# Moving four small copy groups on ScalarE behind a pair's exponentials in a fused attention, state-space and expert kernel

## The reference

```
Q = (x_text @ Wq) as 4 heads of 32;  K = (x_vision @ Wk) as 4 heads of 32
scores = Q K^T / sqrt(32)                       # per head 128 x 2048
topv, topi = top_k(scores, 32)
attn = softmax(topv) scattered to topi, zero elsewhere
attn_mean = attn.mean(over heads)               # 128 x 2048 per batch
c_t = attn_mean @ (x_vision @ Wv)               # 128 x 512 per batch
x = layernorm(x_text) * (1 + g * scale(c_t)) + g * shift(c_t)
y = s4d(x, ...)                                 # a convolution, its kernel computed from dt, A, C
```

## Time and profile before

| | |
|---|---|
| median of 3 runs | 776.59 us (776.24 to 779.22) |
| the profiled execution, device time | 776.36 us |
| its span, first to last instruction | 774.5 us |
| mean granted TensorE clock | 0.916 of full |
| busy: PE, DVE, ACT, POOL | 676.0, 366.7, 268.4, 234.1 us |
| PE busy in 84 to 115, 157 to 187, 187 to 209 us | 17.75 of 31, 25.71 of 30, 10.83 of 22 us |
| PE busy in 300 to 774 us | 449.78 of 474 us |

### The profile page before, as it was taken

How to read it: one execution, slowest core, us unless ns; L and a number is a source line. 1 busy time by engine, 2 the same in 40 slices (tenths; PEclk the granted TensorE clock), 3 DMA queues, 4 the chain that set the end, 5 groups by cost and what they waited for, 6 DMA issues and landing times.

```text
span 774.5 us, 10077 instructions
## 1 busy us (share of the span) xinstructions
PE 676.0 (87%) x3848; PEld 316.6 (41%) x3848; DVE 366.7 (47%) x1179; ACT 268.4 (35%) x564; POOL 234.1 (30%) x146
## 2 busy tenths in 40 slices
PE   4967669888378799999999999999699999999997
PEld 1423235334244354444444444455544333333343
DVE  5998769978998235570003350534661111001114
ACT  1866868779688110013210002444111001111010
POOL 2499668858977910000000000000140000000012
PEclk9977676868569999999999999999699999999999
DMA  9971320802706750014014023002958999999924
GB/s 296 289 271 52 108 83 2 271 1 76 291 0 222 213 239 19 1 41 176 0 50 167 0 82 135 1 1 74 361 201 311 389 379 344 373 373 371 384 81 135
DMA packets 63521, 132.94 MB, mean 172 GB/s; under 512 B 8368, under 2 KB 18544, under 8 KB 62960
## 3 DMA queue, kind: packets, MB, share of 16 engines
q1 hardware_dynamic: 59072, 122.91, 44.1%
q0 software_dynamic: 1920, 6.29, 2.8%
q10 hardware_dynamic: 2480, 3.08, 1.2%
HBM read 121.86 MB, written 8.32 MB: 168 GB/s over the span
## 4 chain that ended last, share of the span: by engine, by line
PE 67%; ACT 10%; DVE 7%; POOL 6%; DMA 4%; issue 3%; SPq 2%; DVEq 0%; POOLq 0%
PE PS L1696 7%; PE PS L1671 7%; PE PS L1492 7%; PE PS L1512 7%; PE PS L1410 6%; PE PS L1264 4%; PE PS L1529 4%; PE PS L1691 4%; PE PS L1676 4%; PE PS L1297 3%; DMA AR<-in_ctxT 3%; DVE AR L1010 2%; PE PS L1314 2%; PE PS L1526 2%; SPq L290 2%
## 5 line engine op out<-in xcount | busy, mean ns | idle before, releaser
L422 POOL TENSOR_TENSOR RS<-VE,CST 128x1 f32<-128x1 f32 (+1 forms) x18 | 11.2, 623 | 267.6 <-DVE VE L919 265.3
L1297 PE MATMUL PS<-AR,WK 128*128 128x512 f32 x96 | 55.8, 738 | 17.2 <-DMA AR<-in_ctxT 17.1
L956 DVE MAX8 KA<-AR 128x8 f32<-128x64 f32 x512 | 66.4, 211 | 0.8 <-ACT AR L607 0.8
L1235 DVE COPY AR<-PS 128x512 f32<-128x512 f32 (+1 forms) x9 | 5.9, 668 | 124.3 <-PE PS L1264 124.3
L574 POOL DMA_INDIRECT AR<-expert_rows,SLU x8 | 8.4, 1050 | 180.9 <-DMA expert_rows<-XT 178.8
L1696 PE MATMUL PS<-AR,TT 128*32 128x512 f32 x512 | 59.5, 593 | 1.4 <-issue 1.3
L1314 PE MATMUL PS<-AR,QT 32*128 32x512 f32 x128 | 45.1, 790 | 16.8 <-ACT AR L607 13.5
L1671 PE MATMUL PS<-AR 128*32 128x512 f32 x512 | 58.0, 594 | 1.1 <-ACT AR L870 0.6
L1492 PE MATMUL PS<-TT,AR 128*128 128x512 f32 (+2 forms) x144 | 55.5, 546 | 3.3 <-ACT TT L798 3.3
L1410 PE MATMUL PS<-AR 128*128 128x512 f32 x128 | 56.1, 594 | 0.9 <-ACT AR L770 0.6
L1512 PE MATMUL PS<-AR 128*128 128x512 f32 x128 | 55.5, 593 | 0.9 <-ACT AR L807 0.9
(11 more groups left out here) (293 smaller groups left out, 1197.4 us busy)
## 6 DMA issues: line engine op xcount, KB each, us to landing
AR<-in_w SPq DMA_DIRECT2D x32, 2048.0 KB, 12.4
AR<-in_ctxT SPq DMA_DIRECT2D x16, 768.0 KB, 7.6
AR<-in_ctx SPq DMA_DIRECT2D x16, 768.0 KB, 7.8
AR<-in_W SPq DMA_DIRECT2D x2, 4096.0 KB, 12.9
token_rows<-AR SPq DMA_DIRECT2D x1, 2560.0 KB, 10.1
X<-in_x SPq DMA_DIRECT2D x2, 1024.0 KB, 5.5
AR<-AR POOLq DMA_DIRECT2D x8, 256.0 KB, 3.4
AR<-in_W_film_in SPq DMA_DIRECT2D x4, 512.0 KB, 10.5
```

The costliest lines, as they stand in the source:

```text
L956: last = eng.max(CAND[i % 2][:, n, :], s[:, n * G // NCH:(n + 1) * G // NCH])
L1297: last = mm(PS[:, 4 + n % 2, :], WK[:, j, :], CXT[slot][:, j, :], start=j == 0, stop=j == KV - 1)
```

## The change

ScalarE's code is changed, no other engine's. In the even rounds 2, 4 and 6 the copies of the next batch's key chunks 2 and 3 stood at the round's end, and in rounds 4 and 6 `attended(q - 2)` followed them. Both now stand in the odd round that follows, behind that round's exponentials and ahead of its score copies. Round 0 keeps its two key copies where they were. `attended(2)`, in round 7 behind the magnitudes, stays too. No instruction is added or taken away.

```diff
                 if 2 <= m:
                     exponentials(m - 1)
                 if late:
+                    if q and q + 1 < B:
+                        context_keys(q + 1, (2, 3))
+                    if q >= 2:
+                        attended(q - 2)
                     if m + 1 < NPH:
                         scores(m + 1, (0, 1))
...
                         step_turns(q)
                     else:
                         exponentials(0)
-                    if q + 1 < B:
-                        context_keys(q + 1, (2, 3))
                     if m == 0:
+                        context_keys(1, (2, 3))
                         for b in range(1, B):
                             text_columns(b, (5, 7)[b % 2])
...
                         link(eng.activation(TM[:, :], TM8[:, :], ACT.Copy))
-                    if q >= 2:
-                        attended(q - 2)
```

## The result

| | before | after |
|---|---|---|
| median of 13 runs each | 776.73 us (775.36 to 779.24) | 780.29 us (779.32 to 783.3) |
| ratio, 95% interval | | 1.0047 [1.0036, 1.0057] |
| profiled execution, device time / span | 776.36 / 774.5 us | 782.19 / 780.4 us |

The changed kernel is slower by 0.47%, some 3.6 us, where 1.7 us were forecast. The sign was right and the time lies inside the stated range, but the loss is twice the forecast.

A forecast was written before the change was run, and what follows sets the result against it. TensorE was taken to bound the kernel, with ScalarE on the path in rounds 3, 5 and 7. -1.3 + 3.3 - 0.3 = +1.7 us on 776.36 gave 778.1; own range 776.9 to 779.4, wider 774.8 to 780.6.

The forecast's parts named there:

- Round 3, -1.3: Round 3: exponentials start earlier without the key copies ahead of them, a gain of 1.3 us.
- the two cases of the prediction, 0.83 and 1.71: Round 3: gain of 0.83 us with the eight transposes at the low clock, 1.71 at the high one.
- the bound of 2.44: Round 3: the most it can give, 2.44 us, VectorE's wait for the exponentials ahead of its masking.
- Round 5, +3.3: Round 5: TensorE waits at the CC transposes, then runs scores and transposes at the low clock, 3.3 us later.
- Round 7, -0.3: Round 7: masking starts 0.35 us earlier, the sines still wait for GpSimd, later copies stay hidden; gain 0.3 us.
- a sign that it is wrong: Round 7: the last exponentials waiting for L642 would show the prediction wrong.
- with 0.2 to spare: Round 7: L642 ends at 236.55, ahead of the last exponentials at 236.77, so it stays hidden.
- a context product that keeps the low clock longer: Round 7 rival: context product at the low clock longer outlasts its 0.2 us cover, 780.5 us; chance 0.14.
- The rest, 0: Outside the three rounds: no DMA moved, instruction counts and durations unchanged, no term in the sum.

The follow-up runs named there:

- e1: Changed kernel with TensorE's CC transposes of batches 0 and 1 moved behind the next pair's first scores; 0.9979 of the kernel before.
- e2: Changed kernel with only the key copies moved, `attended` back at its old place ahead of the exponentials; 0.9999 of the kernel before.
- e6: Changed kernel with round 5's CC transposes behind the first scores and batch 1's attended context back ahead of the exponentials; 0.9956 of the kernel before.
- e4: Changed kernel with 20 unused products in TensorE's idle time of round 5, ahead of the CC transposes; 0.9977 of the kernel before.
- e5: Changed kernel with batch 1's attended context back ahead of the exponentials, so round 7 is ordered as before; 1.0019 of the kernel before.
- e7: Changed kernel with three tiny VectorE instructions ahead of round 7's masking of head 12, to start it later; 1.0044 of the kernel before.
- e8: Changed kernel with 20 unused TensorE products in round 5 and batch 1's attended context back ahead of the exponentials; 0.9946 of the kernel before.
- e9: e8 with 10 more unused products in TensorE's idle time of round 3; 0.9962 of the kernel before.
- e3: Changed kernel with only `attended` moved, the key copies back at their old place ahead of the exponentials; 1.0063 of the kernel before.

## Why the prediction was right or wrong, step by step

- **Round 3, -1.3.** Measured -0.84 to -0.87 in both profiles of the changed kernel and in e1, e2 and e6; in e4, e5 and e7, with the same order at this place, it was -1.58 to -1.71. These are the two cases of the prediction, 0.83 and 1.71, one for each level of the clock at the eight transposes. A value between them, near the mean that I took, came only in e8 (-1.43), where the level fell in the midst of the transposes (1.38 us). With the clock held (e9) it is -2.56, where GpSimd binds, as the bound of 2.44 had it.
- **Round 5, +3.3.** Measured +3.1. The step itself, that TensorE waits at the CC transposes and then does in a row at the low clock what it did beside the exponentials, was right to 0.2 us: 164.09 for the transposes against 165.03 less the 0.94 that round 3 had given. One piece of its evidence was none: behind the wait of 5.37 us in the earlier trace rows stood only transposes that were not ready either, so it couldn't show that TensorE keeps its order. The 5.16 us in the changed kernel do, with scores standing ready behind them, which e1 runs at once when they stand first. e1, e3 and e4 show that order and clock make it together: the order alone taken away gives 4.2, the clock alone 6.1.
- **Round 7, -0.3.** This step failed. It measured +0.85 and +0.50 up to the last exponentials, and 0.9 more behind them. The last exponentials followed L642 directly, which the prediction had named as a sign that it is wrong. The prediction let the masking gain 0.35 and gave every instruction its old length, "with 0.2 to spare". But that gain (0.47 us against the subtraction, from 0.30 behind to 0.17 ahead) put the masking first, the subtraction became 2.05 longer, and the sines that were to wait for GpSimd as before waited for a later GpSimd. e5 and e7 show it. Of the two figures +0.50 is the one with the CC transposes at the high clock, +0.85 the one with them at the low. The rival that I had put at this place, a context product that keeps the low clock longer, was not the cause: the product took 10.59 us in the first profile, at the high clock, and 12.82 in the second, whose last exponentials came sooner.
- **The rest, 0.** In the profiles 0.9 and 2.7 us more passed from the last exponentials to the last context product. 0.9 of it is the change: it lies ahead of the last transposes (24.2 against 23.3), comes from the later swap, and is gone in e5 and e7. The other 1.8 of the first profile are the clock, 1.0 ahead of those transposes and 0.8 at them. So the term was not 0 but the second half of round 7's.
- **Sum.** -0.9 + 3.1 + 0.5 + 0.9 = +3.6, as by the medians; with the clock of the first profile at the CC transposes it is 0.35 more, and the level at other places moves single executions by a microsecond or two. Of the 1.9 us that the forecast missed, round 7 with what follows from it makes 1.7 and round 3 0.4, less 0.2 that round 5 was costed too high.
- **The range.** The forecast's own range ended at 779.4 and was missed. The time lies in the wider one, up to 780.6, which had been drawn for a rival with another cause (the context product's clock, 780.5). That it held is luck.

## What to carry to other kernels

When a copy is moved behind a long instruction, look for what waits for it on the other engine and what stands behind that waiter in its order: there the price is paid, and moving the waiter behind the independent work (e1) turned +0.39% into -0.21%. An idle time on TensorE can cost twice, once itself and once in the clock of what follows (round 5 here: 5.16 us idle, then a row that took 11.9 us instead of the 6.2 of e4). And a duration read beside another engine's work is not a constant: a shift of less than 0.5 us changed which of two engines was stretched, so a move that shifts the start of one of them past the other's has to be costed with the two lengths exchanged, and followed as far as anything waits for the later one.

## What the runs showed of the hardware

- VectorE's masking (128x2048, two SBUF operands) and GpSimd's subtraction (128x1024) took turns in round 7: the one that starts first keeps its pace (2.34 or 2.35 us), the other takes about 2 us longer (4.40 instead of 2.35, 4.20 instead of 2.34) and ends some 2.2 us after the first. A lead of 0.17 us was enough for the masking (after), 0.24 for the subtraction (e7).
- TensorE at the low clock did not return to the high one in 13 us of scores, mask products and transposes without a gap (164.09 to 177.93 in the changed kernel, granted clock 0.50 throughout); the same work, started at the high clock, kept it (e4). The context product behind it brought the clock to 0.90 in the stretch 182 to 184.
- Products without use, 4.5 us of them in TensorE's idle time (e4), brought the changed kernel from a ratio of 1.0039 and 1.0047 in its own groups to 0.9977 in e4's.
